# Attention-output stage of a graph-attention and expert network on one Trainium2 core: one normalised row for two norms, double-buffered rows, weight loads at other places

## What is computed

```python
x = x + gnn(layernorm(x), ...)          # attention over a graph of 6250 nodes and 100000 edges
x = x + experts(layernorm(x), ...)      # top 2 of 8 experts; x: [6250, 256]

def layernorm(x, eps=1e-05):
    m = mean(x, axis=-1); v = var(x, axis=-1)
    return (x - m) / sqrt(v + eps)

# the end of gnn, for each node: weighted sum of source rows over heads, divided by the sum of the weights
attn = ex / maximum(denom[dst], 1e-10)
out = segment_sum(h_src * attn, dst) + bias

# the beginning of experts, xt = layernorm(x):
logits = xt @ Wr + br                   # softmax, top 2 of 8
mu, var = mean(xt), var(xt)
xn = (xt - mu) * rsqrt(var + 1e-05)     # a second norm, of the row that is already normalised
h = gelu(einsum(xn * ln_g + ln_b, W1) + b1);  y = einsum(h, W2) + b2
```

## Time and profile before

| | us |
|---|---|
| median of 3 runs (lowest, highest) | 2456.93 (2450.55, 2460.57) |
| profiled execution: its own time | 2452.51 |
| profiled execution: span | 2450.7 |
| mean granted TensorE clock, share of full speed | 0.945 |
| last sum of `edges` on VectorE begins | 1355.66 |
| `attend`: first and last VectorE instruction begin | 1356.88, 1506.04 |
| `route` begins on ACT | 1509.12 |
| `experts`: first gather begins | 1574.28 |

### The profile page before, as it was taken

How to read it: one execution, slowest core, us unless ns; L and a number is a source line. 1 busy time by engine, 2 the same in 40 slices (tenths; PEclk the granted TensorE clock), 3 DMA queues, 4 the chain that set the end, 5 groups by cost and what they waited for, 6 DMA issues and landing times. The chain is left out here.

```text
span 2450.7 us, 38965 instructions
## 1 busy us (share of the span) xinstructions
PE 2197.2 (90%) x10372; PEld 1497.0 (61%) x10373; DVE 1595.4 (65%) x3839; ACT 1166.2 (48%) x2772; POOL 1358.8 (55%) x1442
## 2 busy tenths in 40 slices
PE   6589999999999999999998343699999999999997
PEld 4456666666666666666665342566766766676675
DVE  5478888888888888888887797633333333333332
ACT  3357777777777777777776121022212222212221
POOL 2267777777777777777774000044444444444444
PEclk9789999999999999999998555899999999999999
DMA  7545555555555545555552645712221222122121
GB/s 219 171 135 150 150 156 157 158 157 146 153 156 157 155 143 157 155 157 145 153 157 72 227 151 74 230 31 31 33 34 30 34 34 32 32 34 32 32 34 28
DMA packets 154089, 275.35 MB, mean 112 GB/s; under 512 B 37224, under 2 KB 103401, under 8 KB 153706
## 3 DMA queue, kind: packets, MB, share of 16 engines
q0 software_dynamic: 67088, 150.41, 25.5%
q1 hardware_dynamic: 76298, 107.96, 14.3%
q10 hardware_dynamic: 10576, 15.52, 1.8%
HBM read 236.95 MB, written 36.83 MB: 112 GB/s over the span
## 5 line engine op out<-in xcount | busy, mean ns | idle before, releaser
L521 POOL DMA_INDIRECT arena<-h_tab,src x880 | 937.0, 1065 | 337.3 <-issue 250.7
L663 PE MATMUL psum<-arena 128*128 128x256 f32 x1760 | 488.7, 401 | 51.1 <-DVE arena L756 48.9
L684 PE MATMUL psum<-arena 128*128 128x264 f32 x1760 | 477.8, 395 | 8.9 <-DVE arena L774 8.6
L663 PEld LDWEIGHTS psum<-arena 128*128 128x128 f32 x1760 | 302.4, 191 | 226.6 <-issue 83.9
L1346 ACT ACTIVATE arena<-psum 128x512 f32<-128x512 f32 x212 | 115.0, 594 | 673.0 <-PE psum L1324 673.0
L1307 PE MATMUL psum<-arena 128*128 x856 | 386.7, 594 | 2.3 <-DVE arena L1360 2.3
L1336 PE MATMUL psum<-arena 128*128 x1696 | 383.6, 379 | 0.0
L684 PEld LDWEIGHTS psum<-arena 128*128 128x128 f32 x1760 | 323.9, 191 | 88.9 <-issue 36.7
L1336 PEld LDWEIGHTS psum<-arena 128*128 128x128 f32 x1696 | 314.0, 190 | 38.3
L756 DVE SCALAR_TENSOR_TENSOR arena<-arena,a_dst,psum 128x512 f32<-128x512 f32 x440 | 323.7, 736 | 8.9 <-PE psum L663 7.1
L1354 DVE TENSOR_TENSOR arena<-psum,arena 128x512 f32<-128x512 f32 x214 | 137.8, 686 | 285.0 <-PE psum L1307 285.0
(11 more groups left out here) (201 smaller groups left out, 2205.4 us busy)
## 6 DMA issues: line engine op xcount, KB each, us to landing
arena<-rel_list SPq DMA_DIRECT2D x110, 512.0 KB, 4.5
arena<-h_tab,src POOLq DMA_INDIRECT x880
arena<-in_x SPq DMA_DIRECT2D x14, 896.0 KB, 8.7
arena<-in_W ACTq DMA_DIRECT2D x8, 1024.0 KB, 14.6
arena<-in_W SPq DMA_DIRECT2D x8, 1024.0 KB, 12.9
arena<-ea_slots SPq DMA_DIRECT2D x440, 8.0 KB
h_tab<-arena SPq DMA_DIRECT2D x7, 924.0 KB, 4.5
out_rows<-arena SPq DMA_DIRECT2D x7, 896.0 KB, 4.1
```

The source lines that it names most:

```text
L521: pool.indirect_dma_start(rows[:, s % RING, k, :], None, d.h_tab[:, :], bass.IndirectOffsetOnAxis(ap=c.src[:, s * U + k:s * U + k + 1], ax ...
L663: last = nc.tensor.matmul(ps[:, HDT + x, y * UE:(y + 1) * UE], hj[:, (s // 2 * 2 + y) % HJ, x * P:(x + 1) * P], oht[:, half % OT, (u + y) ...
L684: last = nc.tensor.matmul(ps[:, AGG, 0:HS], oh[:, a % OH, k, :], rows[:, a % RING, k, :], start=(k == 0), stop=(k == U - 1))
```

## The change

In `attend`:

- The two norms become one pass. If the first norm's deviation is s1 = sqrt(v + eps), the second norm of the normalised row is (x - m) / s2 with s2 = sqrt(v (1 + eps) + eps * eps). Only `xn` is made, by ACT, as an activation with a scale and a bias for each row. The router's logits are made from `xn` and multiplied by s2/s1 (`l_scale`) after the last group. There is one set of statistics and one merge a group.
- The rows of x and the rows of `xn` have two buffers each. The graph stage's bias is added to the loaded rows of x by GpSimd, ahead of VectorE's addition. VectorE's work on the attention rows of group i + 1 stands between the merge and the scales of group i.
- The hardware loops are written out. W1 is loaded by SP in the tail of `edges`; SP loads half of W2 in `attend` (one expert's 1 MB in each of groups 1 to 4), the other half stays in `route`. The ring of gathered rows of `edges` moves up in the arena, out of W1's place. W2 lies in the arena by expert, not by row block.
- Some semaphores of `prepare` and `edges` are merged; their waits stay where they were.

In the diff `mean_of_rows` is L979, L981 and L983; `turn` is the two transposes of a tile and `project` the two matmuls by the router's weights; after the last group VectorE multiplies the logits by `l_scale` and adds `br`.

```diff
 # edges, sync, after its loop
+            sp.wait_ge(hd_done, SLOTS)
+            sp.wait_ge(red_done, NCH)
+            w1 = c.arena[:, W1_AT:W1_AT + W1_WORDS].rearrange("p (k e n) -> p k e n", k=KH, e=X)
+            for e in range(X):
+                sp.dma_start(w1[:, :, e, :], d.W1[e].rearrange("(k p) n -> p k n", p=P)).then_inc(c.w1_loaded, 16)
 # attend
+            load(0)
+            load(1)
+            for i in range(GROUPS):
                 sp.wait_ge(x2_made, i + 1)
+                sp.dma_start(d.out[group(i), :].rearrange("(k p) i -> p k i", p=P), x2[:, i % 2]).then_inc(x2_stored[i % 2], 16)
+                if i + 2 < GROUPS:
+                    sp.wait_ge(x2_stored[i % 2], 16 * (i // 2 + 1))
+                    sp.wait_ge(xn_made, GT * (i + 1))
+                    load(i + 2)
+                if 1 <= i <= X // 2:
+                    sp.dma_start(w2[:, i - 1], d.W2[i - 1].rearrange("(h p) n -> p h n", p=P)).then_inc(c.w2_loaded, 16)
...
+        @block.gpsimd
+        def _(pool):
+            for i in range(GROUPS):
+                pool.wait_ge(x_loaded[i % 2], 16 * (i // 2 + 1))
+                nc.gpsimd.tensor_tensor(x2[:, i % 2], x2[:, i % 2], c.gnn_bias[:, :].unsqueeze(1).to_broadcast([P, GT, IN]), ALU.add).then_inc(biased, 1)
...
+            def deviations(i):
+                act.wait_ge(var_made, i + 1)
+                nc.scalar.activation(sd[:, 0, :], mv[:, 3, :], ACT.Sqrt, bias=c.eps[:, :], scale=1.0 / IN)
+                nc.scalar.activation(sd[:, 1, :], mv[:, 3, :], ACT.Sqrt, bias=eps2, scale=(1.0 + LN_EPS) / IN).then_inc(sd_made, 1)
+            def normalise(i, k):
+                nc.scalar.activation(xn[:, i % 2, k, :], x2[:, i % 2, k, :], ACT.Identity, bias=shift[:, 0, k:k + 1], scale=rs[:, 1, k:k + 1]).then_inc(xn_made, 1)
...
+            for i in range(GROUPS):
+                deviations(i)
+                act.wait_ge(scale_made, 4 * (i + 1))
+                if i >= 2:
+                    act.wait_ge(xn_stored[i % 2], 16 * (i // 2))
                 for k in range(GT):
+                    normalise(i, k)
+                    if k >= 2:
+                        take_xT(i * GT + k - 2)
+                act.wait_ge(xn_made, GT * (i + 1))
+                act.dma_start(d.xn[group(i), :].rearrange("(k p) n -> p k n", p=P), xn[:, i % 2]).then_inc(xn_stored[i % 2], 16)
+                for k in range(GT - 2, GT):
+                    take_xT(i * GT + k)
...
+            for n in range(J):
+                turn(n)
+                if n >= 2:
+                    project(n - 2)
...
+            def add_rows(i):
+                dve.wait_ge(den_step, 3 * i + 3)
+                dve.wait_ge(biased, i + 1)
+                nc.vector.tensor_tensor(x2[:, i % 2], x2[:, i % 2], att.rearrange("p (k i) -> p k i", k=GT), ALU.add).then_inc(x2_made, 1)
...
+            def scales(i):
+                dve.wait_ge(sd_made, i + 1)
+                if i:
+                    dve.wait_ge(xn_made, GT * i)
+                nc.vector.reciprocal(rs, sd).then_inc(scale_made, 1)
+                dve.wait_ge(scale_made, 4 * i + 1)
+                nc.vector.tensor_tensor(shift[:, 0, :], mv[:, 4, :], rs[:, 1, :], ALU.mult).then_inc(scale_made, 1)
+                nc.vector.tensor_tensor(l_scale[:, i * GT:(i + 1) * GT], sd[:, 1, :], rs[:, 0, :], ALU.mult).then_inc(scale_made, 1)
+                dve.wait_ge(scale_made, 4 * i + 2)
+                nc.vector.tensor_scalar(shift[:, 0, :], shift[:, 0, :], -1.0, None, ALU.mult).then_inc(scale_made, 1)
+            mean_of_rows(0)
+            for i in range(GROUPS):
+                add_rows(i)
+                if i + 1 < GROUPS:
+                    mean_of_rows(i + 1)
+                scales(i)
+            dve.wait_ge(logits_made, J)
...
 # route, sync
-            for e in range(X):
+            for e in range(X // 2, X):
...
```

More of the change, by code:

```diff
@@ L484, in edges @@
         hj = take(HJ * HD).rearrange("p (b n) -> p b n", b=HJ)
+        assert at >= W1_AT + W1_WORDS
+        rows = take(RING * U * HS).rearrange("p (r k n) -> p r k n", r=RING, k=U)
         at, end = REST_AT, ARENA
@@ L911, in attend @@
-        sd, rs, sdb, rsb = (take(GT) for _ in range(4))
+        x2, xn = (take(2 * GW).rearrange("p (b k i) -> p b k i", b=2, k=GT) for _ in range(2))
+        xT = take(3 * IN).rearrange("p (b i) -> p b i", b=3)
+        st = take(GT * 6).rearrange("p (k s) -> p k s", k=GT)
+        mv = take(5 * GT).rearrange("p (s k) -> p s k", k=GT)
+        sd, rs, shift = (take(2 * GT).rearrange("p (s k) -> p s k", s=2) for _ in range(3))
+        den = take(GT * H).rearrange("p (k h) -> p k h", k=GT)
+        eps2 = take(1)
@@ L912, in attend, with group, load @@
+        at, end = REST_AT, LOGITS_AT
+        att = take(GW)
+        l_scale = take(J)
         ps = c.psum
         LG = 3
[L914 removed]
+        bank = lambda n: n % 3
         block = ctx.enter_context(nc.Block())
+        def group(i):
+            return slice(i * GT * P, (i + 1) * GT * P)
         @block.sync
         def _(sp):
[L919 to L925 removed]
+            w2 = c.arena[:, W2_AT:W2_AT + W2_WORDS].rearrange("p (e h n) -> p e h n", e=X, n=IN)
+            def load(i):
+                sp.dma_start(x2[:, i % 2], d.x[group(i), :].rearrange("(k p) i -> p k i", p=P)).then_inc(x_loaded[i % 2], 16)
+            load(0)
+            load(1)
+            for i in range(GROUPS):
+                sp.wait_ge(x2_made, i + 1)
+                sp.dma_start(d.out[group(i), :].rearrange("(k p) i -> p k i", p=P), x2[:, i % 2]).then_inc(x2_stored[i % 2], 16)
[5 more added lines that the diff above has]
+                    sp.dma_start(w2[:, i - 1], d.W2[i - 1].rearrange("(h p) n -> p h n", p=P)).then_inc(c.w2_loaded, 16)
+            for b in range(2):
+                sp.wait_ge(x2_stored[b], 16 * ((GROUPS + 1 - b) // 2))
@@ new lines, in project @@
+            def project(n):
+                pe.wait_ge(xT_copied, n + 1)
+                for m in range(KH):
+                    last = nc.tensor.matmul(ps[:, LG, n * X:(n + 1) * X], xT[:, bank(n), m * P:(m + 1) * P], c.wr[:, m, :],
+                                            start=(m == 0), stop=(m == KH - 1))
+                last.then_inc(logits_made, 1)
+            for n in range(J):
+                turn(n)
+                if n >= 2:
+                    project(n - 2)
+            project(J - 2)
```

205 lines of the change are left out of this document (75 added, 130 removed).

## The result

The changed kernel takes 2421.32 us (median of four runs, 2412.41 to 2422.26), the kernel before 2457.6 (2450.55 to 2460.57): ratio 0.9848, 95% interval 0.9817 to 0.988, so 36.3 us less. That is faster, though by less than 2%, and inside the forecast's range, but 12 us above the 2409 forecast. The loop through the buffers did set the pace, as in the likeliest case, but longer than forecast, because rival (2) was there too: GpSimd and VectorE excluding each other, which had the smaller chance. That the time meets rival (2)'s 2421 to 2425 is in part luck: its mechanism gave 10.6 us where 12 to 16 were priced, a longer tail added some 9 more than forecast, and a shorter start and edge loop gave 6 back.

The account below looks back on a forecast made before the run. VectorE's work list was taken to bound `attend`, then the loop through two buffers of x. 2452.5 - 47.2 (`attend`) + 2.5 (gathers) - 1.0 (`experts`' first gather) = 2406.8, plus half of 4.4: 2409 us; range 2394 to 2430.

Parts of the forecast that it names:

- the likeliest case: `attend`: the loop through the buffers of x sets the pace, 12 to 14 us a group, 2409 us in all; chance 0.47.
- rival (2): `attend`: GpSimd costs more than its own time, excluding VectorE's two-SBUF-input operations; 12 to 16 us, 2421 to 2425; chance 0.28.
- VectorE's list: `attend`: VectorE's own work per group falls to 8.8 us in place of 19.12.
- The loop through two buffers: `attend`: reusing a buffer of x takes 24.7 us plus 1.5 for SP's queue, 26.2 for two groups.
- ACT's term: `attend`: up to a group's last `xn`, ACT's seven rows and four copies take 4.4 us, bounds 4.0 and 6.0.
- A(0): `attend`: VectorE's addition of x in the first group starts at 9.0 us, 5.0 for the load and 4.0 for the bias.
- A(6): `attend`: VectorE's addition of x in the last group starts at 87.6 us; 16.0 and 0.8 follow to the end.
- three signs of being wrong: New profile: VectorE additions beyond 2.03 us while GpSimd works, additions evenly 9 us apart, or a tail longer by more than 6.
- Rival (3): `attend`: VectorE stays the pace at 8.8 to 10.5 us a group, stage 80 to 95, kernel 2387 to 2399; chance 0.15.
- Rival (4): Tail of `edges`: the last gathers queue behind all of W1, landing 21 us later, kernel 2428; chance 0.06.
- Rival (5): `attend`: GpSimd's bias so slow that the kernel is slower than before, gain used up at 15.3 us; chance 0.04.
- W1 in the tail: Tail of `edges`: W1's loads delay the last gathers by 2.5 us, bounds 0 and 5.6.

Follow-up runs that it names:

- run 11: Changed kernel with one buffer for the rows of x instead of two; 1.0083 of the kernel before, `attend` 178.6 us.
- run 2: Changed kernel with the bias addition back on VectorE and GpSimd left out of `attend`; 0.9779 of the kernel before, `attend` 97.2 us.
- run 3: Changed kernel with all of W2 loaded in `route`, none in `attend`; 0.9865 of the kernel before, `attend` 113.7 us.
- run 8: Changed kernel with three buffers of x, bias on VectorE and scales ahead of the next attention rows; 0.9741 of the kernel before, `attend` 91.0 us.
- run 1: Changed kernel with W1 issued later in the tail, after VectorE's last logits; 0.9855 of the kernel before, tail 37.5 us, `attend` 110.1.
- runs 8 and 12: Changed kernel with three buffers, bias on VectorE, scales first, run twice; 0.9741 and 0.9757 of the kernel before, tails 28.7 and 38.4 us.
- run 10: Kernel before with W1's loads alone moved into the tail, the ring moved up for it; 0.9978 of the kernel before, `attend` 142.8 us.
- run 6: Changed kernel with W1's loads back on ACT's queue in `attend`; 0.9829 of the kernel before, `attend` 116.5 us, tail 28.7.
- run 7: Changed kernel with three buffers of x and three experts' W2 loaded in `attend`; 0.9783 of the kernel before, `attend` 99.6 us.
- run 4: Changed kernel with VectorE's scales ahead of the next group's attention rows; 0.9828 of the kernel before, `attend` 107.3 us.
- run 5: Changed kernel once more, unedited, on another chip; 0.9843 of the kernel before, `attend` 115.0 us, tail 37.2.

## Why the prediction was right in its range and wrong in its case

**VectorE's list: right.** A group without interference is 8.4 us (addition to last scale, in run 11), forecast 8.8.

**The loop through two buffers: the right structure, mis-sized.** It was to be 24.7 and 1.5 for SP's order, 26.2 for two groups; it was 28.0, 30.0 and 28.8. Summed over the three pairs, and read from the changed kernel's timelines:

| step of the loop, three pairs | forecast | measured | difference |
|---|---|---|---|
| addition to the last scale | 26.4 | 35.9 | +9.5 |
| ACT until the load is issued | 13.2 | 16.5 | +3.3 |
| load, with its handover | 22.8 | 22.2 | -0.6 |
| bias on GpSimd, to the addition | 11.7 | 12.3 | +0.6 |
| order on SP's queue | 4.5 | 0 | -4.5 |
| sum (of unrounded rows) | 78.6 | 86.8 | +8.2 |

The step that failed is the first: that VectorE's list keeps its length while GpSimd works. It was longer by 3.7 us in the first addition and by 3.5 in each of the two 7-column instructions, 10.6 us in all, which more than fills the 9.5. Runs 2 and 11 show it from the other side: no GpSimd beside VectorE, no such instruction. ACT's term failed smaller: 4.4 us for seven rows holds only if no copy makes them wait, and from the fourth row on ACT goes at TensorE's 1.17 us a tile, which the prediction had let hide under VectorE's 8.8 a group. The 1.5 us for the order on SP's queue was not there: the next load was issued within 0.1 us of ACT's last row in all three pairs, and run 3 gives at most 1.3 us for all of W2 in the whole stage.

**GpSimd's price: right.** 3.96 to 3.99 us undisturbed, forecast 3.9. But its price for the stage is not its duration: leaving GpSimd out (run 2) won 17.8 us, though VectorE then does the work itself.

**The stage's ends.** A(0) came at 9.3 (forecast 9.0; what held its addition up is in the loop's first term), and from A(6) to the end it took 18.9 (forecast 16.0 and 0.8): the seven tiles through ACT and TensorE took 10.8 where I had 8.3. Together with the loop: 115.0 instead of 104.4.

**The rivals.** Rival (2) was priced at 3.9 in the first addition and 3.9 in two or three later places, 12 to 16 us, 2421 to 2425; it happened at three places, 10.6 us. Its rule stood in the Trainium skill, its price was worked out, and I gave it 0.28 since no row of the trace bore on it. Two of the three signs of being wrong that the prediction named came: an addition on VectorE of 5.70 us, and a tail longer by more than 6. Rival (3)'s range has a slip: its stage of 80 us gives 2384 by the prediction's own sum, not 2387, which changes nothing here. Rival (3) is what run 8 makes of the kernel: VectorE sets the pace, at 11.14 us, once all three obstacles are gone. Rival (4) did not occur: the last gather came 4.1 us later, not 21. Rival (5), a slow bias, did not occur; but run 11 shows that the loop it spoke of, gone round once a group instead of once a pair, does make the kernel slower than before.

**W1 in the tail: +2.5 forecast, +4.1 measured, inside its bounds of 0 to 5.6.** The 4.1 is the difference of two profiles with W1 in flight in one of them (DMA share 1.01 at 1320 to 1330); no experiment could repeat it. The other 7.5 us of the tail's 11.6 are the clock's and a step that the forecast did not have: it took the tail's clock as given. On the first chip TensorE's stop at the fall of the clock was longer with W1, 6.85 us instead of 2.70; whether that kept the clock low to the end isn't shown. In the later sessions it is not settled as W1's effect: run 1 had the low clock with W1 late, and runs 8 and 12, one and the same kernel, had one of each. What stays open is whether W1's transfers make the low clock likelier. Of eleven profiles with W1 in the tail, six had it to the tail's end and run 2's for some 3 us; of three without, none to the end and one in part. On the first chip the changed kernel's highest and lowest runs (2422.26 at a mean clock of 0.947, 2412.41 at 0.953) lie about as far apart as the two kinds of tail do; that the tail is the cause is argued from the size alone.

**W1 out of `attend`.** I had counted the 5.25 us wait inside the 152.2. Run 10 gives W1's move alone 9.7 us there. In the changed kernel run 6 gives it 1.5, less than one profile can tell; there the loop sets the pace.

**W2 and b1.** The first gathers of `experts` fell from 4.5 to 3.3 us, the forecast -1; in `experts` as a whole (875 to 880 us in all runs) that can't be seen.

**The sum.** Against the profiled time: `attend` -37.2 (forecast -47.2), tail +11.6 (+2.5), the stages behind +1.2 (-1), the start and the edge loop -6.4 (0), together -30.7 (-45.7). Of the 15 us missing, 10 are `attend`'s, 9 the tail's, 2 the stages' behind; the shorter start and edge loop gave 6 back.

## What to carry to other kernels

Before moving work from VectorE to GpSimd, look at what VectorE runs meanwhile: if it has two SBUF inputs, or is a float32 `tensor_scalar` (seen once here), the two exclude each other, and the duration of GpSimd's instruction lands on VectorE's, even on one of 7 columns. In a profile this is no wait; look for an instruction that is far longer than its kind and ends when the other engine's does. When buffers go round a loop, write down every link (compute, last reader, store, load, what prepares the data): each is paid once a round, so a third buffer (-15.4 us), an order that frees the buffer sooner (-7.6, of which some 3 by phase) and one engine less in the loop (-17.8) were each worth more than where W2 is loaded (1.3 at most). And before believing a stage difference of a few us from one profile, see how far the stage moves in a run that does not touch it: here it was 5.

## What the runs showed of the hardware

The exclusion was seen on additions and multiplications of two tensors, on `SCALAR_TENSOR_TENSOR` (3.92 us on 7 columns, run 7), and on `TENSOR_SCALAR` with one input (3.91 us, run 4); batch statistics ran beside GpSimd's addition in their usual 2.38 us (run 7), and a reciprocal of 14 columns in its usual 0.23 (1407.32 in the changed kernel). For the one-input case the Trainium skill ("SBUF — State Buffer", who interferes with whom) counts `tensor_scalar` among the operations that can enter a mode using both ports and then exclude GpSimd; run 4's instruction agrees with that, though the trace does not show the mode.

ACT's activation of 256 columns with a bias and a scale for each row takes 0.60 us, and three back to back take 1.59, so 0.50 each, against 0.508 and 0.43 assumed back to back.

In the two first profiles TensorE's clock fell from 1.00 to 0.50 at a stop of TensorE (2.70 and 6.85 us). In the later ones there was no such stop, TensorE was busy for some three quarters of the time (8.88 of 12 us in run 5, 8.91 in run 8), and the clock fell 9 to 13 us into the tail in some executions and not in others, of one and the same kernel too. It set the tail at 37.2 to 38.4 us instead of 28.7 to 29.2 (30.0 in run 2, with some 3 us at 0.50). The edge loop of this program took some 160 us longer in all three later sessions than in the first profiles, while `attend` of one kernel differed by less than 1 us.
